# A post-norm two-layer transformer step: layer 1's expert weights loaded earlier, the down product two experts behind, and the slot table built tile by tile

## The reference

```python
Q, K, V = heads(x @ qw + qb), heads(x @ kw + kb), heads(x @ vw + vb)
feature_map = lambda t: jax.nn.elu(t @ fw1 + fb1) @ fw2 + fb2
KV, Z = einsum('bhsf,bhsd->bhfd', feature_map(K), V), feature_map(K).sum(axis=2)
```

```python
h = silu(buf @ w_gate) * (buf @ w_up)        # per expert: buf 96 x 512, weights 512 x 192
out = h @ w_down                             # 192 x 512
y = segment_sum(out[se, pos] * w, tok)       # weighted, added to the token's row
result = y + silu(x @ ws_gate) * (x @ ws_up) @ ws_down   # shared expert
```

## Time and profile before

| | |
|---|---|
| median of 3 runs | 1588.38 us (1587.12 to 1590.78) |
| the profiled execution, its own time | 1585.73 us |
| span in its profile, first to last instruction | 1583.9 us |
| mean granted TensorE clock | 0.926 of 2.4 GHz |
| busy: PE, DVE, ACT, POOL | 85%, 68%, 46%, 48% |
| moved by DMA | 212.68 MB, 134 GB/s over the span |
| keys of layer 1 | about 694 to 870 us |
| shared stage of layer 1 | 1129 to 1232 us |
| routed stage of layer 1 | 1239 to 1534 us |
| last combine | 1544 to 1583.9 us |

### The profile page before, as it was taken

How to read it: one execution, slowest core, us unless ns; L and a number is a source line. 1 busy time by engine, 2 the same in 40 slices (tenths; PEclk the granted TensorE clock), 3 DMA queues, 4 the chain that set the end, 5 groups by cost and what they waited for, 6 DMA issues and landing times. The chain is left out here.

```text
span 1583.9 us, 21495 instructions
## 1 busy us (share of the span) xinstructions
PE 1347.1 (85%) x7253; PEld 1110.7 (70%) x7253; DVE 1078.5 (68%) x1795; ACT 730.1 (46%) x1158; POOL 759.9 (48%) x654
## 2 busy tenths in 40 slices
PE   5999859999599999946999789998897799999950
PEld 5787647767377777735899679987666577777740
DVE  5688757232388888865886556666395588888847
ACT  4121032000188888832454354444221588888840
POOL 1455520000388887833664323332274467777734
PEclk9899979999799999977999789999997899999985
DMA  4000040000366567632110000002422999999958
GB/s 167 1 1 27 27 134 2 1 0 0 132 222 212 175 186 251 234 120 54 49 54 2 10 28 1 1 1 100 155 86 108 334 338 338 341 340 339 336 145 318
DMA packets 81808, 212.68 MB, mean 134 GB/s; under 512 B 20426, under 2 KB 23498, under 8 KB 79292
## 3 DMA queue, kind: packets, MB, share of 16 engines
q1 hardware_dynamic: 50075, 133.14, 23.2%
q0 software_dynamic: 31120, 77.38, 17.4%
q10 hardware_dynamic: 528, 1.05, 0.2%
HBM read 208.75 MB, written 46.79 MB: 161 GB/s over the span
## 5 line engine op out<-in xcount | busy, mean ns | idle before, releaser
L66 PE MATMUL bank<-e_w_hi,e_xt_hi 128*96 128x384 f32 (+1 forms) x444 | 168.4, 379 | 3.1 <-DVE e_w_lo L2700 3.1
L68 PE MATMUL bank<-e_w_hi,e_xt_lo 128*96 128x384 f32 (+1 forms) x444 | 160.8, 362 | 0.0
L67 PE MATMUL bank<-e_w_lo,e_xt_hi 128*96 128x384 f32 (+1 forms) x444 | 160.7, 362 | 0.0
L1064 POOL DMA_INDIRECT e_w_raw<-in_w_gate_up,r_load_of x47 | 54.6, 1161 | 215.5 <-issue 215.5
L2590 POOL DMA_INDIRECT sums<-e_y,r_target_of x64 | 108.4, 1694 | 73.1 <-DMA sums<-e_y,r_target_of 41.6
L1189 DVE TENSOR_TENSOR e_w_lo<-e_w_raw,e_w_hi 128x2048 fp32r<-128x2048 f32 x47 | 107.7, 2292 | 33.9 <-ACT e_w_hi L1148 26.3
L2700 DVE TENSOR_TENSOR e_w_lo<-r_w_early,e_w_hi 128x1536 fp32r<-128x1536 f32 x48 | 84.8, 1767 | 25.9 <-ACT e_w_hi L2664 24.9
L231 POOL TENSOR_TENSOR a_read<-a_read_n 128x256 f32<-128x256 f32 x64 | 50.2, 785 | 103.7 <-DVE a_read_n L452 103.7
L1056 POOL DMA_INDIRECT e_xg<-rows,r_token_of x47 | 91.5, 1947 | 14.3 <-issue 14.3
L1757 POOL TENSOR_TENSOR q_g_lo<-q_gf,a_g 128x512 fp32r<-128x512 f32 x32 | 41.6, 1301 | 112.2 <-ACT a_g L1921 112.2
L1148 ACT ACTIVATE e_w_hi<-e_w_raw 128x2048 fp32r<-128x2048 f32 x47 | 89.8, 1910 | 0.0
(11 more groups left out here) (481 smaller groups left out, 4463.2 us busy)
## 6 DMA issues: line engine op xcount, KB each, us to landing
r_w_early<-in_w_gate_up SPq DMA_DIRECT2D x48, 768.0 KB
r_w_early<-in_w_down SPq DMA_DIRECT2D x24, 768.0 KB
results<-e_y SPq DMA_DIRECT2D x47, 256.0 KB
rows<-resid SPq DMA_DIRECT2D x8, 1024.0 KB, 4.4
r_w_first<-in_w_gate_up SPq DMA_DIRECT2D x8, 768.0 KB
r_low<-in_w_down SPq DMA_DIRECT2D x8, 768.0 KB
e_w_raw<-in_w_gate_up SPq DMA_DIRECT2D x8, 768.0 KB
resid<-in_x SPq DMA_DIRECT2D x4, 1024.0 KB, 5.5
```

The lines of the kernel that those rows point to most:

```text
L66: pe.matmul(out, a_hi, b_hi, start=start, stop=False)
L67: pe.matmul(out, a_hi, b_lo, start=False, stop=False)
L68: return pe.matmul(out, a_lo, b_hi, start=False, stop=stop)
L1064: pool.indirect_dma_start(w1_raw[p][:, :], None, io["w_gate_up0"], bass.IndirectOffsetOnAxis(k.load_of[:, c:c + 1], 0), bounds_check=E0 * ...
```

## The change

It has four parts.

1. **Turned rows by chunk.** `xt_hi` and `xt_lo` become one tile, chunk by chunk (chunk, half, block, 512 tokens), read through the class `TurnedRows`. A chunk's part is free once its `gate_up` steps are done.
2. **Loads and table in the shared stage.** The freed chunks and tiles 0 to 11 of `k.x` become slots: gate and up weights of ten experts and five pairs of down weights are issued in the shared stage, each when its place is free (`s_gu` at 2, 4 and 6; the row stores `s_sums0`, now one semaphore a chunk). The row stores of `sums0` are spread between them. `at_col` is no longer made at once: `table()` makes it per tile by six `tensor_scalar` of 64 columns, in a ring; both rings have NR = 6. PE's `prefix()` comes after `gate_up(4)`, in front of `down(1)`, not after `gate_up(5)`. POOL gathers three experts' rows at the end, not four.
3. **Routed stage.** A new helper `pipeline` takes each stage with its own distance. PE: `turn` 1 ahead, `gate_up`, `turn_hidden` 1 behind, `down` 2 behind. ACT does the silu before the copy of the down rows (`down_hi`), DVE the product before the low part (`down_lo`), and each `hidden` turn comes after the next `gate_up`. 12 gate-up slots and 6 down slots, loads 10 ahead; gathered rows in a ring of 6, fetched 5 ahead; additions 2 behind.
4. **Keys.** `tile(0)` moves from the first round of the loop to between `combine(4)` and `combine(5)`, `keys(2)` in front of `normalise(2)`.

```diff
+def pipeline(eng, n, unroll, *stages):
+
+    def step(g):
+        for stage, ahead in stages:
+            if 0 <= g + ahead < n:
+                stage((g + ahead) // unroll, (g + ahead) % unroll)
...
+class TurnedRows:
+    def __call__(self, b, first, n):
+        c, at = first // CH, first % CH
+        return self.both[:, c, self.half, b, at:at + n]
...
             combine(4)
+            tile(0)
             combine(5)
             rstd(2)
+            keys(2)
             normalise(2)
-            for i in range(NT):
+            combine(6)
+            turn(4)
+            for i in range(1, NT):
...
+    k.w1_early = [k.w1_first[:, :, :]] + [gate_up_of(a) for a in (unit(1), unit(2), unit(3), unit(5), unit(6), unit(8), unit(9), resid(1), resid(2))]
+    k.w2_early = [down_of(a) for a in (unit(0), unit(4), unit(7), resid(0), resid(3))]
...
-        NR = 3
+        NR = 6
         at_row = [sb(f"at_row{n}", [P, K1, CAP], F32R) for n in range(NR)]
+        at_col = [sb(f"at_col{n}", [P, K1, E1], F32R) for n in range(NR)]
...
                 def gate_up_and_routes(u):
                     gate_up(u)
-                    if u == 5:
+                    if u == 4:
                         prefix()
...
-                    vec.wait_ge(k.s_sums1, 16 * (NC + 2))
-                    shape = [P, NT, K1, E1]
-                    step(vec.tensor_tensor(at_col[:, :, :, :], codes.unsqueeze(1).unsqueeze(1).to_broadcast(shape),
-                                           code_top[:, :, 0:K1].unsqueeze(3).to_broadcast(shape), ALU.is_equal))
...
                         if i >= NR:
                             vec.wait_ge(s_used, i - NR + 1)
+                        for kk in range(K1):
+                            mark = vec.tensor_scalar(at_col[i % NR][:, kk, :], codes, code_top[:, i, kk:kk + 1], tok[:, i:i + 1],
+                                                     ALU.is_equal, ALU.mult)
+                        mark.then_inc(s_col, 1)
...
     with ExitStack() as ctx:
-        U, NX = 8, 4
+        U, NX, NR = 12, 4, 6
...
-                for e in range(4):
+                for e in range(3):
...
-                for g in range(-2, E1 + 1):
-                    if g + 6 < E1:
-                        gather((g + 6) // U, (g + 6) % U)
...
+                for g in range(-2, E1 + 2):
+                    if g + 5 < E1:
+                        gather((g + 5) // U, (g + 5) % U)
...
-                three_stages(pe, E1, turn, gate_up, down, between=turn_hidden, unroll=U)
+                pipeline(pe, E1, U, (turn, 1), (gate_up, 0), (turn_hidden, -1), (down, -2))
...
-                three_stages(act, E1, turned_hi, silu, results, between=hidden_hi, prepare=weights_hi, unroll=U)
+                pipeline(act, E1, U, (turned_hi, 1), (weights_hi, 1), (silu, 0), (hidden_hi, -1), (down_hi, 0), (results, -2))
...
-                three_stages(vec, E1, turned_lo, hidden, nothing, between=hidden_lo, prepare=weights_lo, unroll=U)
+                pipeline(vec, E1, U, (turned_lo, 1), (weights_lo, 1), (hidden, 0), (hidden_lo, -1), (down_lo, 0))
```

More of the change, by code:

```diff
@@ L513, in three_stages @@
     for g in range(unroll * rounds + 1, n + 1):
+        step(g)
+def pipeline(eng, n, unroll, *stages):
[3 more added lines that the diff above has]
+                stage((g + ahead) // unroll, (g + ahead) % unroll)
+    first, last = -max(ahead for _, ahead in stages), -min(ahead for _, ahead in stages)
+    rounds = (n + first - 1) // unroll
+    for g in range(first, 2 * unroll + 1):
+        step(g)
+    with eng.Fori(2, rounds) as i:
+        for q in range(unroll):
+            for stage, ahead in stages:
+                stage(i + (q + 1 + ahead) // unroll, (q + 1 + ahead) % unroll)
+    for g in range(unroll * rounds + 1, n + last):
         step(g)
@@ L1217, with __init__ @@
 CODE_BASE, CODE_STEP = 1 << 23, 1 << 12
+class TurnedRows:
+    def __init__(self, both, half):
+        self.both, self.half = both, half
+    def __call__(self, b, first, n):
+        c, at = first // CH, first % CH
+        return self.both[:, c, self.half, b, at:at + n]
 def attention1(k):
@@ L1235, in attention1 @@
         fw2_t = sb("fw2_t", [P, 2 * FM])
-        xt = tuple(k.sb("a1_xt_" + n, [P, KD, T], F32R, ctx) for n in ("hi", "lo"))
+        both = sb("xt", [P, NC, 2, KD, CH], F32R)
+        xt = tuple(TurnedRows(both, half) for half in range(2))
         w = {"fw1_hi": sb("fw1_hi", [P, 4 * FM], F32R), "fw1_lo": sb("fw1_lo", [P, 4 * FM], F32R),
@@ L1550, in turn @@
                     vec.wait_ge(s_thi, n + 1)
-                    part = lambda a: a[:, 2 * half:2 * half + 2, c * CK:(c + 1) * CK]
+                    part = lambda a: a(slice(2 * half, 2 * half + 2), c * CK, CK)
                     vec.tensor_tensor(part(xt_lo), bank[0][:, :].rearrange("p (b t) -> p b t", b=2), part(xt_hi), ALU.subtract).then_inc(s_tlo, 1)
@@ L2088, in experts1_shared @@
     k.target_of = rt("target_of", [CAP, E1], I32)
-    k.s_sums0, k.s_sums1 = k.sem("e1_first_sums_begun"), k.sem("e1_second_sums_begun")
+    k.s_sums0, k.s_sums1 = [k.sem(f"e1_first_sums_begun{c}") for c in range(NC)], k.sem("e1_second_sums_begun")
     k.w1_first = rt("w1_first", [P, KD, 2 * F1])
@@ L2340, in _ @@
                     act.wait_ge(s_tps, b + 1)
-                    act.activation(xt_hi[:, b, c * CH:(c + 1) * CH], bank[b % 2][:, :], ACT.Copy).then_inc(s_thi, 1)
+                    act.activation(xt_hi(b, c * CH, CH), bank[b % 2][:, :], ACT.Copy).then_inc(s_thi, 1)
                 act.wait_ge(s_lg, 1)
@@ L2527, in experts1_routed @@
         mine = lambda p: slice(2 * (p % 2), 2 + p % 2)
-        xg = k.xg_early + k.xg_low + [k.sb(f"e1_xg{p}", [CAP, D + E1], F32, ctx)[:, :] for p in range(6, U)]
+        xg = (k.xg_early + [k.sb(f"e1_xg{p}", [CAP, D + E1], F32, ctx)[:, :] for p in range(3, NR)]) * (U // NR)
         xt_hi, xt_lo = two("xt_hi", [P, KD * CAP], F32R), two("xt_lo", [P, KD * CAP], F32R)
@@ L2556, in load @@
                 def load(h, p):
-                    if not past(h, p, 6):
+                    if not past(h, p, 10):
                         return
@@ L2671, in hidden_hi, with down_hi @@
                     act.activation(ht_hi[p][:, :], bank[4 + p % 2][:, 0:2 * CAP], ACT.Copy).then_inc(s_hh, 1)
-                def silu(h, p):
+                def down_hi(h, p):
                     e = U * h + p
@@ L2678, in silu @@
                     act.activation(w2_hi[p][:, mine(p), :], w2_raw[p][:, mine(p), :], ACT.Copy).then_inc(s_vhi, 1)
+                def silu(h, p):
+                    e = U * h + p
                     act.wait_ge(s_gu, e + 1)
```

139 lines of the change are left out of this document (77 added, 62 removed).

## The result

The changed kernel takes 1583.38 us (median of 16 runs, 1576.47 to 1586.73), the kernel before 1587.03 beside it (16 runs). The ratio is **0.9967, 95% interval 0.9956 to 0.9979**: 5 us faster, where 29 were forecast. The profiled execution, the slowest of the 16 (1586.73 us), spans 1.1 us more than that of before, so places are compared here by their own lengths, not by when they begin.

What follows compares the result with a forecast made beforehand. In the routed experts PE and the DMA engines were both taken as near their limit, at 4.46 us an expert. Gains 3 + 16 + 10 = 29 us take 1585.7 to 1556.7, median 1559; own range 1554 to 1565, full range 1547 to 1572.

Steps and rivals of the forecast that it cites:

- Keys: Start of the keys: tile 0 and keys 2 fill PE's 8.34 us hole; gain 3 us, bounds 0 and 5.
- Slot table: Shared stage: DVE's two wide instructions go, six narrow ones a tile come, routed stage begins sooner; gain 16 us.
- I take 0.14: Slot table: 0.14 us for each 64-column DVE instruction, upper bound 0.25, lower 0.08.
- Rival 3: Shared stage: table slow at 0.25 us an instruction, POOL held up beside it; gain 23, 1565 to 1574 us; chance 0.08.
- The stage's end: Shared stage ends with POOL's last gather; three gathers, not four, save 1.2 us; routed stage begins at 1222.4, not 1238.8.
- Loads: Shared stage: ten gate-up and five down loads issued there, none on a path; gain 0, less to move later.
- Down two behind: Routed stage: hidden turn gets 2.15 us more cover, PE runs at about 4.23 us an expert; gain 10, bounds 1 and 15.
- I take 4.36: Routed stage: the chain of additions, 4.45 us an expert before, taken at 4.36 as PE asks for 4.23.
- Rival 4: Routed stage: deeper queue of weight loads slows every addition, deciding from 9.43 us a pair; slower, 1592 us; chance 0.05.

Runs made afterwards that it cites:

- `low_in_four`: The changed kernel with DVE's low part of gate and up in four instructions of 384 columns instead of one of 1536: 1573.75 us, ratio 0.9917.

## Why the prediction was wrong

The kernel is faster, as forecast, but by 5 us and not 29, and most of what it gained came from a part that I had priced at 0.

- **Keys**, forecast 3 us: 2 in the trace, 2 alone (at the edge of what can be told). The fifth turn moved 7.3 us later against the first one (6 were told), and the sixth followed 3 us on.
- **Slot table**, forecast 16 us: 4.0, and all of it behind the gathers. Two steps failed. *The size*: "I take 0.14" for a narrow instruction; it is 0.24, almost the upper bound of 0.25 that the single row gave. I had taken the value from the overlap of wide ones. The Trainium skill's 0.094 (VectorE: DVE Perf Modes, The perf-mode tier table) was farther off still. *The mechanism*: I costed DVE alone and let POOL's products lie "beside". POOL's sixteen wide instructions hold DVE up by 15.8 us. Rival 3 had the slow instruction, and POOL held up; it did not have DVE held up. The trace had shown the mirror image, 7.61 us of POOL beside DVE's wide instruction, and I used it only as a gain. The GPSIMD Engine Reference of the Trainium skill (Specifications), which I cited against the change, was right. Some 3 us of the missing 12 are no property of the change. PE's granted clock is 0.67 of its upper level, 2.4 GHz, from 1150 to 1160 us in this profile. Five other kernels have the same code up to the routed stage: the three with a granted clock of 1.00 there took 97.5 to 97.8 us, the two with 0.66 and 0.71 took 100.5 and 100.7.
- **The stage's end**: I let it end with POOL's last gather and the same 9.63 us (from 1203.5 my own terms give 1223.1 and not 1222.4, which leaves the gain at 16). It is 4.50 now; that gap had been the gathers' landing beside the weight loads, as the DMA shares above have it.
- **Loads**, forecast 0, "None is on a path": they were. The 5.1 us at the stage's end are put down to moving them sooner, and without these the shared stage would have gained nothing in this profile. No wait for a weight load is left in the routed stage, as told.
- **Down two behind**, forecast 10 us: -3.7. The hidden turn's wait is gone and PE ran at 4.1 while it could. The step that failed is "**I take 4.36**" for the chain: I let the additions quicken because PE asked for more. Their pair is a sum of issue and rest, and its rest is 7.1 to 7.5 us in every two-chain run. With the new order and the short issue (`low_in_four`) the pair is 8.86, that of before: without a quicker addition the order gains nothing in the middle of the stage, only at its end. And the issue is not fixed either: it grew by 0.65 us, since in the changed kernel DVE's 1.76 us instruction stands on top of it. Over some fifty steps 4.71 instead of 4.36 is 17 us; the end gives part of it back, where additions catch up (13 steps at 3.40).
- **Rival 4** named the right place and the right sign for the stage, a pair above 9.4 us, with the wrong cause: the load queue, which grew no deeper. That its sign came is luck. Its time, 1592, did not come since the shared stage and the end gave back.
- **Sum** in the profile: +1.4 ahead of the keys and +1.1 between keys and shared stage, in code that is the same or nearly so, -2.0 in the keys, -4.0 in the shared stage, +3.7 in the routed stage, +1.5 to the last addition (1532.93 became 1534.61) and -0.6 in the last combine make +1.1, as the spans have it. The medians say -3.7, the ratio of the runs -5. The 3 us at the lower clock are the likely part of that difference.

## What to carry to other kernels

When a chain of dependent transfers paces a loop, write its period as issue plus landing, and ask which of the two a reordering touches; another engine that could run faster does not shorten it. More slots are not a deeper queue: count the loads that wait. Where POOL issues transfers or computes beside DVE, count for each wide instruction of the one a hold-up of the other, and see whether it falls on work that someone waits for; cutting DVE's long instruction in four cost it 0.2 us an expert and gave 8 to 10 us in all where it stood on the additions, and lost 4 us in the kernel where it did not. A trace shows only one phase of such a loop: after a reorder the same hold-ups may fall elsewhere.

## What was unexpected of the hardware

- The hold-up goes both ways. A narrow DVE instruction, 0.30 us alone, took up to 1.43 us beside one of POOL of 1.3 us; a POOL issue of 1.44 us that begins inside DVE's 1.76 us takes up to 3.0, and ends 1.3 us after DVE's. In these traces who began first goes on, and the other waits for its end.
- An addition's rest hardly depends on how many weight loads wait, as long as there are some: 7.13 us with 2.9 loads waiting on average (the changed kernel), 7.26 with 5.9 (`low_in_four`). With none outstanding the time from issue to landing fell from 9.2 to 5.3 us (1500 to 1520 us of the changed kernel).
- The DMA engines gave 336 to 343 GB/s from 1300 to 1480 us in every kernel here. With two chains and twelve slots the loads end early and the engines have little left to do (101 GB/s from 1500 to 1520 us of the changed kernel).
